# tanh into PSUM, a scan that reads its addends there, and h copied into them by chunk

## The reference, cut to what matters

```
x = x + linear(x * cond) * d                    # a modulated linear layer, 8 x 256 x 256
for t in range(256):                            # a GRU over the time steps, h: 8 x 256
    Z = sigmoid(xz[t] + H @ Whz.T + bhz)
    R = sigmoid(xr[t] + H @ Whr.T + bhr)
    G = tanh(xh[t] + (R * H) @ Whh.T + bhh)
    H = Z * H + (1 - Z) * G
    Y[t] = H @ Whq.T + bhq
x = x + Y
```

## Time and profile before

| | us |
|---|---|
| median of 3 runs | 642.17 (641.68 to 643.65) |
| the profiled execution | 641.54 |
| its span, from the first to the last instruction | 639.7 |
| PE busy | 626.1 |
| VectorE (DVE) busy | 490.9 |
| ScalarE (ACT) busy | 209.2 |

### The profile page before, as it was taken

The page is one execution under the profiler, slowest core; times in us unless marked ns, Lnnn a source line. Parts: engine busy times, 40 slices in busy tenths (PEclk is TensorE's granted clock), DMA queues, the critical chain, the costliest instruction groups (busy, mean ns, idle before and its releaser), DMA issues.

```text
span 639.7 us, 39673 instructions
## 1 busy us (share of the span) xinstructions
PE 626.1 (98%) x16826; PEld 567.4 (89%) x16826; DVE 490.9 (77%) x4047; ACT 209.2 (33%) x1607; POOL 4.5 (1%) x11
## 2 busy tenths in 40 slices
PE   8999999999999999999999999999999999999986
PEld 3689999999999999999999999999999999999875
DVE  5788877777877778787777777777787777777775
ACT  3133333333333332333333333333333333333322
POOL 2000000000000000000000000000000000000000
PEclk9955555555555555555555555555555555555555
DMA  7000000000000000000000000000000000000000
GB/s 263 3 4 3 11 6 4 13 4 12 4 5 12 5 12 4 12 5 4 13 4 12 4 13 4 5 12 5 12 5 4 13 4 13 5 12 4 4 12 11
DMA packets 6629, 8.84 MB, mean 14 GB/s; under 512 B 818, under 2 KB 4914, under 8 KB 6452
## 3 DMA queue, kind: packets, MB, share of 16 engines
q1 hardware_dynamic: 5872, 6.03, 2.9%
q10 hardware_dynamic: 580, 0.28, 0.2%
HBM read 4.21 MB, written 2.10 MB: 10 GB/s over the span
## 4 chain that ended last, share of the span: by engine, by line
PE 93%; DVE 4%; ACT 1%; DMA 1%; issue 1%; DVEq 0%
PE chunk_bank L625 53%; PE z_rec_bank L625 13%; PE chunk_bank L617 12%; PE z_bank L617 6%; PE y_bank L602 6%; PE chunk_bank L634 1%; DMA x<-x_cm 1%; PE chunk_bank L554 1%; DVE lin L367 1%; PE y_bank L560 1%; DVE r_hidden L490 1%; DVE hidden L534 1%; DVE r_hidden L494 0%; DVE r_hidden L498 0%; ACT scan_mul L316 0%
## 5 line engine op out<-in xcount | busy, mean ns | idle before, releaser
L625 PE MATMUL chunk_bank<-r_hidden,w_part 128*128 128x8 bf16 x6144 | 206.3, 169 | 0.2
L625 PEld LDWEIGHTS chunk_bank<-r_hidden,w_part 128*128 128x128 bf16 x6144 | 184.8, 105 | 18.3 <-issue 0.6
L625 PEld LDWEIGHTS chunk_bank<-hidden,w_part 128*128 128x128 bf16 x3072 | 102.4, 104 | 36.0 <-DVE hidden L534 7.4
L625 PE MATMUL chunk_bank<-hidden,w_part 128*128 128x8 bf16 x3072 | 125.0, 173 | 6.2 <-DVE hidden L534 6.2
L534 DVE TENSOR_TENSOR_SCAN hidden<-scan_mul,hidden 128x24 f32<-128x24 f32 x512 | 80.5, 199 | 60.6 <-ACT hidden L319 54.3
L316 ACT ACTIVATE scan_mul<-z_pre 128x16 f32<-128x16 f32 x256 | 57.2, 223 | 197.2 <-DVE z_pre L502 197.2
L625 PE MATMUL z_rec_bank<-hidden_parts,w_part 128*128 128x24 bf16 x3072 | 121.5, 181 | 0.1
L625 PE MATMUL chunk_bank<-hidden_parts,w_part 128*128 128x8 bf16 x3072 | 119.2, 168 | 0.0
L314 ACT ACTIVATE r_bank<-chunk_bank 128x8 f32<-128x8 f32 x256 | 41.5, 162 | 212.1 <-PE chunk_bank L625 206.6
L625 PEld LDWEIGHTS z_rec_bank<-hidden_parts,w_part 128*128 128x128 bf16 x3072 | 103.2, 104 | 0.2 <-DVE z_rec_bank L449 0.2
L625 PEld LDWEIGHTS chunk_bank<-hidden_parts,w_part 128*128 128x128 bf16 x3072 | 102.9, 104 | 0.0
(11 more groups left out here) (80 smaller groups left out, 656.8 us busy)
## 6 DMA issues: line engine op xcount, KB each, us to landing
x<-x_cm SPq DMA_DIRECT2D x4, 512.0 KB, 8.1
out_cm<-result SPq DMA_DIRECT2D x16, 128.0 KB, 2.1
w_rec<-w_rec_cm SPq DMA_DIRECT2D x1, 768.0 KB, 8.4
w_in<-w_in_cm SPq DMA_DIRECT2D x1, 768.0 KB, 9.9
w_mod<-w_mod_cm ACTq DMA_DIRECT2D x1, 256.0 KB, 5.5
w_out<-w_out_cm SPq DMA_DIRECT2D x1, 256.0 KB, 10.4
cond<-cond_cm ACTq DMA_DIRECT2D x1, 8.0 KB, 1.7
bias_rows<-gate_bias ACTq DMA_DIRECT2D x1, 4.0 KB
```

What stands on the lines that cost most here:

```text
L625: return nc.tensor.matmul(cols, w_part[wp][:, gate, k, m * P:(m + 1) * P], moving, start=first, stop=True, skip_group_check=True)
```

## The change

The second half of `hidden`'s columns goes. The addends of the scan now lie in PSUM, in 24 columns of the bank that holds the gate area of the chunk and step (`scan_add`): tanh writes columns 1, 4, ... of them (L319), and VectorE writes h twice, into columns 0, 3, ... and 2, 5, ..., with one copy for each chunk (`feed_scan`) behind `split_h`, in place of L349. The scan reads its addends there. Each R sigmoid waits for the copy of its chunk (`scan_fed`), a wait that is written ahead of the one for `pre_r`. The first pair of copies stands ahead of the loop, behind `take_z(0, m)`. In j = 8, 9 of the blocks from 1 on the bank for chunk 1 is now `z_bank`. `finish`, `take_z`, `add_x` and `first_x1_rest` change their steps, and ahead of the copies of j = 3 and 7 there are waits for `y_ready` and `z_ready`.

```diff
--- before.py
+++ after.py
@@ -114,7 +114,7 @@
 
 
         PART = 3 * B
-        hidden = sb("hidden", [P, KC, SLOTS, 2 * PART])
+        hidden = sb("hidden", [P, KC, SLOTS, PART])
         hidden_parts = sb("hidden_parts", [P, KC, SLOTS, PARTS, B])
         r_hidden = sb("r_hidden", [P, KC, PARTS, B])
         z_pre = sb("z_pre", [P, KC, B])
@@ -156,10 +156,18 @@
         y_bank = pb("y_bank")
         r_bank = pb("r_bank")
 
-        def r_gate(k, n, j):
-
-            bank = r_bank if k == 0 else (z_bank if n > 0 and j < 4 else y_bank)
-            return bank[:, KC * BC:KC * BC + B]
+        def step_bank(k, t):
+
+            n, j = t // BLOCK, t % BLOCK
+            return r_bank if k == 0 else (z_bank if n > 0 and (j < 4 or j in (8, 9)) else y_bank)
+
+        def r_gate(k, t):
+
+            return step_bank(k, t)[:, KC * BC:KC * BC + B]
+
+        def scan_add(k, t):
+
+            return step_bank(k, t)[:, KC * BC + 2 * B:KC * BC + 2 * B + PART]
 
         def lin_bank(i, m):
 
@@ -221,6 +229,7 @@
         pre_z = sem("pre_z")
         h_ready = [sem(f"h_ready{k}") for k in range(KC)]
         h_packed = sem("h_packed")
+        scan_fed = [sem(f"scan_fed{k}") for k in range(KC)]
         h_rest = [sem(f"h_rest{k}") for k in range(KC)]
         h_rest2 = [sem(f"h_rest2{k}") for k in range(KC)]
 
@@ -310,13 +319,14 @@
             for t in range(T):
                 p, j, n = t // BLOCK % 2, t % BLOCK, t // BLOCK
                 for k in range(KC):
+                    act.wait_ge(scan_fed[k], t + 1)
                     act.wait_ge(pre_r[k], t + 1)
-                    nc.scalar.activation(r_gate(k, n, j), pre(p, R, k, j, j + 1), ACT.Sigmoid).then_inc(r_ready[k], 1)
+                    nc.scalar.activation(r_gate(k, t), pre(p, R, k, j, j + 1), ACT.Sigmoid).then_inc(r_ready[k], 1)
                 act.wait_ge(pre_z, t + 1)
                 nc.scalar.activation(scan_mul[:, :, 2::3], z_pre[:, :, :], ACT.Sigmoid, scale=-1.0)
                 for k in range(KC):
                     act.wait_ge(pre_g[k], t + 1)
-                    nc.scalar.activation(hidden[:, k, (t - 1) % SLOTS, 3:3 + PART:3], pre(p, G, k, j, j + 1),
+                    nc.scalar.activation(scan_add(k, t)[:, 1::3], pre(p, G, k, j, j + 1),
                                          ACT.Tanh).then_inc(g_ready[k], 1)
                 if t + 1 < T:
                     seed_z((t + 1) // BLOCK % 2, (t + 1) % BLOCK)
@@ -346,7 +356,13 @@
                     nc.vector.tensor_tensor(h_word(k, slot, 2), h_word(k, slot, 1), h_parts(k, slot, 1, 2), ALU.subtract
                                             ).then_inc(h_rest2[k], 1)
                 nc.vector.tensor_copy(h_word(every_chunk, slot), h_scanned(every_chunk, slot)).then_inc(h_packed, 1)
-                nc.vector.tensor_copy(hidden[:, :, slot, 4:4 + PART:3], h_scanned(every_chunk, slot))
+
+            def feed_scan(t):
+
+                for k in range(KC):
+                    nc.vector.tensor_copy(scan_add(k, t).rearrange("p (b i) -> p b i", i=3)[:, :, 0::2],
+                                          h_scanned(k, (t - 1) % SLOTS).unsqueeze(2).to_broadcast([P, B, 2])
+                                          ).then_inc(scan_fed[k], 1)
 
             nc.vector.memset(zeros[:, :], 0.0).then_inc(zeros_ready, 1)
             dve.wait_ge(ld_cond, 16)
@@ -451,6 +467,8 @@
             seed.then_inc(z_seeded, 1)
             for m in range(KC):
                 take_z(0, m)
+            dve.wait_ge(lin_ready, 3)
+            feed_scan(0)
             dve.wait_ge(ld_bq, 16)
             dve.wait_ge(scan_set, 1)
 
@@ -487,7 +505,7 @@
                     weight_split(6 + j % 2, 1 + (j - 4) // 2)
                 for k in range(KC):
                     dve.wait_ge(r_ready[k], t + 1)
-                    nc.vector.tensor_tensor(r_hidden[:, k, 0, :], r_gate(k, n, j), h_scanned(k, before),
+                    nc.vector.tensor_tensor(r_hidden[:, k, 0, :], r_gate(k, t), h_scanned(k, before),
                                             ALU.mult).then_inc(rh_ready[k], 1)
                 for k in range(KC):
                     dve.wait_ge(rh_ready[k], t + 1)
@@ -503,12 +521,12 @@
                     z_pre[:, :, :], z_rec_bank[:, 0:KC * Z_GROUPS * B].rearrange(
                         "p (m g b) -> p m b g", m=KC, g=Z_GROUPS),
                     axis=mybir.AxisListType.X, op=ALU.add).then_inc(pre_z, 1)
-                if n > 0 and j in (4, 5):
-                    finish(n - 1, j - 4)
-                if n + 1 < NB and j in (8, 9):
-                    if j == 8:
+                if n > 0 and j in (8, 9):
+                    finish(n - 1, j - 8)
+                if n + 1 < NB and j in (12, 13):
+                    if j == 12:
                         dve.wait_ge(z_ready, n + 1)
-                    take_z(1 - p, j - 8)
+                    take_z(1 - p, j - 12)
                 if n == 0 and j < 4:
                     if j == 0:
                         dve.wait_ge(linp_ready, GROUPS)
@@ -517,24 +535,30 @@
                     if j == 3:
                         mul.then_inc(lin_ready, 1)
                 if NB // GROUPS <= n + 2 < NB:
-                    if j == 10:
+                    if j == 4:
                         dve.wait_ge(lin_ready, GROUPS)
+                    if j in (4, 5):
+                        add_x(j - 4, slice((n + 2) * BC, (n + 3) * BC)).then_inc(x1_ready, 1)
+                if n + 2 < NB:
                     if j in (10, 11):
-                        add_x(j - 10, slice((n + 2) * BC, (n + 3) * BC)).then_inc(x1_ready, 1)
-                if n + 2 < NB:
-                    if j in (12, 13):
-                        if j == 12:
+                        if j == 10:
                             dve.wait_ge(x1_ready, x1_count(n + 2))
-                        first_x1_rest(n + 2, j - 12)
+                        first_x1_rest(n + 2, j - 10)
                     if j in (14, 15):
                         second_x1_rest(n + 2, j - 14)
 
                 for k in range(KC):
                     dve.wait_ge(g_ready[k], t + 1)
                     nc.vector.tensor_tensor_scan(hidden[:, k, t % SLOTS, 0:PART], scan_mul[:, k, :],
-                                                 hidden[:, k, before, 2:2 + PART], 0.0, ALU.mult, ALU.add
+                                                 scan_add(k, t), 0.0, ALU.mult, ALU.add
                                                  ).then_inc(h_ready[k], 1)
                 split_h(t % SLOTS, t + 2)
+                if t + 1 < T:
+                    if n > 0 and j == 3:
+                        dve.wait_ge(y_ready, n)
+                    if 0 < n < NB - 1 and j == 7:
+                        dve.wait_ge(z_ready, n + 1)
+                    feed_scan(t + 1)
 
             for k in range(KC):
                 finish(NB - 1, k)
```

## The result

| | before | changed |
|---|---|---|
| median, us | 641.92 (641.04 to 643.65, 4 runs) | 656.83 (654.49 to 657.55, 4 runs) |
| ratio, 95% interval | | 1.0219 (1.0198 to 1.0239) |
| profiled execution, us | 641.54 | 657.37 |
| its span, us | 639.7 | 655.6 |

The changed kernel is slower, by 14.9 us in the medians and 15.8 in the profiled executions. The forecast was 655.2 within 648 to 669.

What follows compares the result with a forecast made beforehand. Latency around the loop of each step was taken to bound the kernel. From 641.54 us, +17.9 (event), -4.6 (tanh) and +0.4 (first copies) gave 655.2 us, slower by 2.1%, within 648 to 669.

Steps and rivals of the forecast that it cites:

- What bounds: Step loop: latency around the closed loop bounds, 2.37 us per step, 256 times, 607 us of the 641.
- Part 4: R sigmoids on ScalarE: the later wait, pre_r, becomes an event inside the loop, +0.07 us per step, +17.9 us.
- Part 1: Tanh on ScalarE writing PSUM instead of SBUF: 18 ns less per step, -4.6 us.
- Part 2: Scan on VectorE reading its addends in PSUM: no price for the source, 0 us.
- Part 3: VectorE's copies into the addends: covered in the loop, +0.4 us once for the first pair ahead of it.
- Part 5: Pieces moved to other steps: cost 0; 3 us if one piece came to lie over the scan.
- A: Rival: the event on pre_r is not in the loop or costs nothing, 637.3 us; chance 0.12.
- B: Rival: the event is cheap, 0.01 to 0.03 us, and cancels against the tanh, 642 us; chance 0.05.
- C: Rival: second R sigmoid falls over 0.11 us behind the first, an event standing between them, 668 us; chance 0.10.
- D: Rival: the scan is 54 ns slower reading from PSUM, 669 us; chance 0.07.

Runs made afterwards that it cites:

- changed and shifted: The changed kernel with two tiny sigmoids added on ScalarE in the preparation: 652.14 us, ratio 1.0166.
- pre_r first and shifted: The changed kernel with pre_r's wait written ahead of scan_fed's and two tiny sigmoids added on ScalarE in the preparation: 637.85 us, ratio 0.9939.
- pre_r first: The changed kernel with the wait for pre_r written ahead of the wait for scan_fed: 640.18 us, ratio 0.9975.
- before_three_waits: The kernel before with three already satisfied waits written ahead of each wait for pre_r: 679.91 us, ratio 1.0596.

## Why the prediction was right

The distances from first scan to last (605.57 before, 618.44 changed, 615.40 changed and shifted, 600.06 pre_r first and shifted) take the change apart:

| term | predicted | measured | from |
|---|---|---|---|
| event on pre_r | +17.9 | +15.3 | 615.40 - 600.06 |
| tanh, scan, copies, pieces | -4.6 | -5.5 | 600.06 - 605.57 |
| ScalarE's long steps and the rest of the shift | not seen | +3.0 | 618.44 - 615.40 |
| copies ahead of the loop | +0.4 | 0 | see below |
| pace of the first fp32 products | not seen | +3.0 | not the change's |

The measured terms add up to the 15.8 of the profiled executions. Part of that agreement is luck. The terms that the forecast had come to 9.8 us where it gave 13.7: the event was priced 2.6 too high, the gain of the rest 0.9 too low, the start 0.4 too high. Two terms that it had not seen, 6.0 us together, brought the sum back to 15.8. The mechanism and the sign do not hang on this. Of the third line 2.16 us are the long steps.

**What bounds** held: each hundredth put into the loop came out in the step, on three engines. The signs named ahead came too: the first sigmoid 0.80 behind the R products (0.81 was given), and PE's weight loads for the G products idle 35.9 us in all, by the page, instead of 18.3.

**Part 4, the wait,** decided the sign, and its mechanism held as told: the later wait becomes the event. With the order of the two waits turned, the same change is 0.25% faster than before. The mechanism had been read from line numbers alone. The price read from one row of the same engine, 0.07, is 0.060 per step (15.3 / 256).

**Part 1, tanh:** 18 ns was forecast. In chunk 1 it is 183 to 162 ns; in chunk 0, the one on the loop, 177 to 168. From tanh to scan the step saves 0.011 with pre_r first. From the overheads that the Trainium skill ("Perfetto Trace Analysis", section "Optimizing Scalar/DVE Operations") gives for ScalarE, about 93 ns on SBUF and 51 on PSUM, an estimate is 42 ns. The sign agrees with these runs, the size does not.

**Part 2, the scan from PSUM:** 0 was forecast, and it is 4 ns less in chunk 0 (208 to 204, medians) and 12 in chunk 1 (190 to 178). The same section of the Trainium skill has about 60 ns on SBUF and 125 on PSUM for VectorE, by which an estimate would be 65 ns more. These runs do not show it. Which part of the 0.021 per step is the scan's and which the tanh's was not separated, as both move with one tile.

**Part 3, the copies:** covered in the changed kernel: both end at least 0.11 us ahead of the first sigmoid. The 0.4 us at the start did not come out at the end: r*h of the first step is late by 0.6 once the 3.0 are taken off (27.27 - 3.0 against 23.64), but the first scan is not (27.98 against 27.99), because the preparation's last fp32 products on PE end later than either.

**Part 5** held: nothing. The price that I gave to a piece lying over the scan, 3 us, was too high by a factor of six.

**Rivals.** A was false (512 events, and they cost). B fell with the event's 0.06 us. C did not act with one event, but does with two. D fell with the scan's 204 and 178 ns.

## What to carry to other kernels

A second semaphore wait ahead of an instruction in a latency-bound loop is not free in these kernels, and which one is written first decides: put first the wait that ends last, and let the separate event take the one that is long over. Read from the trace at which lines events stand before adding a wait; it tells which of the waits was split off. And price an added instruction not only in busy time but by where it moves the engine's program.

## What the runs showed of the hardware that was not expected

- ScalarE starts an instruction about 0.25 us late at some places of its program, 256 apart in the changed kernel and a multiple of 128 apart in before_three_waits. Shifting the program by two instructions removed all eight of the changed kernel. It was seen only at an event or up to two instructions behind one; the kernel before has none.
- The first eight fp32 products of the preparation took 6.73 us in one execution and 3.67 in another. Their pace goes with the granted clock, 0.85 us apart at 0.50 and 0.43 at 1.00. A printed 1.00 can stand for a stretch without a clock record, so look where the records begin. What sets the level there is open.
- An event with two waits takes 38 ns and one with a single wait 17 on ScalarE (before_three_waits, changed kernel).
